# Joining the last two stages of an 8-core transformer block: no barrier between them, final-stage buffers cut from four to two, down-projection buffers cut by one

## What is computed

```python
x = x + _layernorm(_L0_attn_ref(_layernorm(x), ...))      # 16 heads of 128, rope, softmax, output projection
x = x + _layernorm(_L0_ffn_ref(_layernorm(x), ...))

def _L0_ffn_ref(x1, ...):
    w_up = dequant4bit(w_up_q, w_up_scale).T               # 2048 -> 8192
    y1 = x1 @ w_up + b_up + x1 @ w_up_lora_a @ w_up_lora_b
    x2 = jax.nn.relu(y1)
    w_down = dequant4bit(w_down_q, w_down_scale).T         # 8192 -> 2048
    y2 = x2 @ w_down + b_down + x2 @ w_down_lora_a @ w_down_lora_b
    return y2
```

## Time and profile before

| | us |
|---|---|
| timed runs (3) | 6494.24, 6898.83, 6917.61; median 6898.83 |
| profiled execution | 6499.66 |
| its span (core 5, the slowest) | 6497.6 |
| spans of the eight cores | 6372.7 to 6497.6 |
| PE busy in the span | 4829.7 (74%) |
| DVE busy | 1799.8 (28%) |
| ACT busy | 1460.6 (22%) |
| stage 7, first L963 matmul to last bias add | about 5232 to 6315 |
| stage 8, first load issued to end | about 6319 to 6497.6 |

### The profile page before, as it was taken

How to read it: one execution, slowest core, us unless ns; L and a number is a source line. 1 busy time by engine, 2 the same in 40 slices (tenths; PEclk the granted TensorE clock), 3 DMA queues, 4 the chain that set the end, 5 groups by cost and what they waited for, 6 DMA issues and landing times.

```text
span 6497.6 us, 61217 instructions; the slowest of 8 cores (6372.7 to 6497.6 us)
## 1 busy us (share of the span) xinstructions
PE 4829.7 (74%) x21121; PEld 1803.6 (28%) x21121; DVE 1799.8 (28%) x2547; ACT 1460.6 (22%) x1556; POOL 841.2 (13%) x1501
## 2 busy tenths in 40 slices
PE   0399599594999996666665365699999599969970
PEld 0144244241222221111111122244444234424430
DVE  4677321173444442222322256000000000000006
ACT  0011000011777774444444000011111100000000
POOL 1011111111122111111111000011111300020000
PEclk9999799797999998878877687899999899989985
DMA  9533533532465567777767533622223422242237
GB/s 246 184 76 77 105 77 77 95 74 47 144 181 163 170 177 160 156 165 165 160 154 156 131 113 114 115 61 73 67 67 73 136 66 82 82 147 83 82 111 277
DMA packets 672701, 794.60 MB, mean 122 GB/s; under 512 B 495824, under 2 KB 562384, under 8 KB 632832
## 3 DMA queue, kind: packets, MB, share of 16 engines
q0 software_dynamic: 117904, 463.41, 27.5%
q1 hardware_dynamic: 549888, 310.51, 18.3%
q10 hardware_dynamic: 4608, 16.78, 0.7%
HBM read 497.39 MB, written 218.24 MB: 110 GB/s over the span
## 4 chain that ended last, share of the span: by engine, by line
PE 61%; DMA 19%; DVE 9%; SPq 3%; POOL 3%; issue 3%; ACT 1%; DVEq 1%; POOLq 0%; ACTq 0%
PE pqk L377 17%; PE pu L873 14%; PE pd L963 14%; DMA sbc<-wdnsc_t 11%; SPq L98 3%; PE ps_s L600 3%; PE po L718 2%; DMA xb<-x_full 2%; PE ps_l L626 2%; PE ps_c L622 2%; PE ps_s L602 2%; DVE linv_sb L641 2%; PE ps_c L624 2%; PE pu L877 1%; ACT pbuf L618 1%
## 5 line engine op out<-in xcount | busy, mean ns | idle before, releaser
L377 PE MATMUL pqk<-wfull,ltb 128*128 128x512 bf16 x5120 | 1111.5, 380 | 407.7 <-DMA ltb<-ln1x_d 407.7
L618 ACT ACTIVATE pbuf<-ps_s,bexp_all 128x1024 bf16<-128x1024 f32 x1024 | 1135.0, 1116 | 809.7 <-PE ps_s L602 809.6
L963 PE MATMUL pd<-wd_sl,h2h 128*128 128x512 bf16 x4096 | 897.8, 383 | 65.9 <-DVE y2b L981 63.9
L873 PE MATMUL pu<-lt,wu_sl 128*128 128x512 bf16 x4096 | 928.4, 380 | 1.0 <-DVE xa_sb L846 1.0
L377 PEld LDWEIGHTS pqk<-wfull,ltb 128*128 128x128 bf16 x5120 | 502.2, 98 | 1016.5 <-issue 416.5
L600 PE MATMUL ps_s<-qtb,ktb 128*128 128x512 bf16 x1024 | 420.4, 411 | 418.9 <-DVE ctxT L650 339.5
L963 PEld LDWEIGHTS pd<-wd_sl,h2h 128*128 128x128 bf16 x4096 | 403.1, 99 | 560.6 <-issue 86.5
L873 PEld LDWEIGHTS pu<-lt,wu_sl 128*128 128x128 bf16 x4096 | 379.6, 98 | 482.3 <-issue 59.3
L622 PE MATMUL ps_c<-pbuf,vtb 128*128 128x512 bf16 x1024 | 401.4, 392 | 132.3 <-ACT pbuf L618 80.5
L718 PE MATMUL po<-wo_sb,ctxT 128*128 128x512 bf16 x1024 | 258.8, 420 | 223.6 <-DMA ob_bc<-ob_r 121.2
L602 PE MATMUL ps_s<-qtb,ktb 128*128 128x512 bf16 x1024 | 413.1, 403 | 0.0
(11 more groups left out here) (118 smaller groups left out, 3193.6 us busy)
## 6 DMA issues: line engine op xcount, KB each, us to landing
iqb<-wupq POOLq DMA_DIRECT2D x64, 1024.0 KB, 7.2
iqb<-wdnq_t POOLq DMA_DIRECT2D x64, 1024.0 KB, 13.4
sbc<-wdnsc_t POOLq DMA_DIRECT2D x128, 512.0 KB, 17.8
wd_sl<-wdn_deq_d SPq DMA_DIRECT2D x512, 128.0 KB, 2.2
xb<-x_full SPq DMA_DIRECT2D x32, 1024.0 KB, 8.7
wup_deq_d<-dqb SPq DMA_DIRECT2D x64, 512.0 KB, 3.0
wdn_deq_d<-dqb SPq DMA_DIRECT2D x64, 512.0 KB, 5.6
h_d<-h2b POOLq DMA_DIRECT2D x256, 128.0 KB, 2.0
```

The costliest lines, as they stand in the source:

```text
L377: last = e.matmul(pp[:], ltb[lp][:, dc * 512 + t1 * 128: dc * 512 + (t1 + 1) * 128], wfull[:, dc * C.D + og * 512: dc * C.D + (og + 1) * 512],
L618: P.ein("s", lambda e, sp=sp, h=h: e.activation(pbuf[sp][:], ps_s[sp][:], AF.Exp, bias=bexp_all[:, h:h + 1], scale=1.0), "sE")
L873: e.matmul(pp[:], wu_sl[wp][:, dc * 512 + hi * 128: dc * 512 + (hi + 1) * 128], lt2[:, dc * C.T_OWN + t5 * 512: dc * C.T_OWN + (t5 + 1) * ...
L963: last = e.matmul(pd[ti][:], h2h[:, hc * TH + ti * 128: hc * TH + (ti + 1) * 128], wd_sl[wp][:], start=first, stop=False)
```

## The change

- The barrier between stages 7 and 8 is taken out. In its place SP waits, ahead of the loads of tile tc, for the store of the last column group of that token tile (`p7_y2_done[tc]`).
- The buffers of stage 8 are allocated ahead of those of stage 7, so that both exist at the same time. To make room, NP8 goes from 4 to 2, the four `lnf` become one, `wd_sl` goes from 4 slots to 3, and `y2b` from 3 buffers to 2.
- The interleave of stage 8 goes from a lag of two to a lag of one.
- The identity matrix is allocated and loaded at the end of stage 2 rather than at the start, and the PE waits for it.

The core of the diff:

```diff
-    ident_sb = st.enter_context(nc.sbuf_tensor("ident_sb", [128, 128], F32))
-    P.dma("g", ident_sb[:], ident[:])
...
     fin = ExitStack()
+    ident_sb = fin.enter_context(nc.sbuf_tensor("ident_sb", [128, 128], F32))
+    dide = P.dma("g", ident_sb[:], ident[:])
...
     P.wait("t", "vE", P.val("vE"))
+    P.wait("t", "dg", dide)
     P.ein("t", lambda e: e.transpose(ntp[:], nmax[:], ident_sb[:]), "tM")
...
+    NP8 = 2
+    p8 = ExitStack()
+    y2t = [p8.enter_context(nc.sbuf_tensor(f"y2t{i}", [128, C.D], F32)) for i in range(NP8)]
+    xnt = [p8.enter_context(nc.sbuf_tensor(f"xnt{i}", [128, C.D], F32)) for i in range(NP8)]
+    lnf1 = p8.enter_context(nc.sbuf_tensor("lnf1", [128, C.D], F32))
+    lnf = [lnf1] * NP8
+    otb = [p8.enter_context(nc.sbuf_tensor(f"otb{i}", [128, C.D], F32)) for i in range(NP8)]
...
-    wd_sl = [p7.enter_context(nc.sbuf_tensor(f"wd_sl{i}", [128, 512], BF16)) for i in range(4)]
-    y2b = [p7.enter_context(nc.sbuf_tensor(f"y2b{i}", [128, 512], F32)) for i in range(3)]
+    wd_sl = [p7.enter_context(nc.sbuf_tensor(f"wd_sl{i}", [128, 512], BF16)) for i in range(3)]
+    y2b = [p7.enter_context(nc.sbuf_tensor(f"y2b{i}", [128, 512], F32)) for i in range(2)]
...
-                wp = w % 4
-                if w - 4 in wd_mm_end:
-                    P.wait("y", "tM", wd_mm_end[w - 4])
+                wp = w % 3
+                if w - 3 in wd_mm_end:
+                    P.wait("y", "tM", wd_mm_end[w - 3])
...
-                if uy - 3 in y2_st:
-                    P.wait("v", fy2[(uy - 3) % 3], y2_st[uy - 3])
-                yb = y2b[uy % 3]
+                if uy - 2 in y2_st:
+                    P.wait("v", fy2[(uy - 2) % 2], y2_st[uy - 2])
+                yb = y2b[uy % 2]
...
+        for ti in range(NTI):
+            uy = (C.OG - 1) * NTI + ti
+            p7_y2_done[th * NTI + ti] = (fy2[uy % 2], y2_st[uy])
         pds.close()
     p7.close()
-    P.barrier()
...
-    NP8 = 4
...
+        sname, sval = p7_y2_done[tc]
+        P.wait("y", sname, sval)
         dy2 = P.dma("y", y2t[p][:], y2_d[tc * 128:(tc + 1) * 128, :], sem=f8l[p])
...
     for tc in range(C.TCO):
         p8_stage1(tc)
-        if tc >= 2:
-            p8_stage2(tc - 2)
-    p8_stage2(C.TCO - 2)
+        if tc >= 1:
+            p8_stage2(tc - 1)
     p8_stage2(C.TCO - 1)
```

More of the change, by code:

```diff
@@ L893, in build_nc @@
         return nc, P, st
+    NP8 = 2
[5 more added lines that the diff above has]
+    otb = [p8.enter_context(nc.sbuf_tensor(f"otb{i}", [128, C.D], F32)) for i in range(NP8)]
+    s24c = [p8.enter_context(nc.sbuf_tensor(f"s24c{i}", [128, 6 * C.OG], F32)) for i in range(NP8)]
+    mv2c = [p8.enter_context(nc.sbuf_tensor(f"mv2c{i}", [128, 2], F32)) for i in range(NP8)]
+    sd1c = [p8.enter_context(nc.sbuf_tensor(f"sd1c{i}", [128, 1], F32)) for i in range(NP8)]
+    rs1c = [p8.enter_context(nc.sbuf_tensor(f"rs1c{i}", [128, 1], F32)) for i in range(NP8)]
+    nb1c = [p8.enter_context(nc.sbuf_tensor(f"nb1c{i}", [128, 1], F32)) for i in range(NP8)]
+    f8l = P.fam("f8l", NP8)
+    f8o = P.fam("f8o", NP8)
     p7 = ExitStack()
@@ L901, in build_nc @@
     xb_sb = p7.enter_context(nc.sbuf_tensor("xb_sb", [C.R, TH], BF16))
-    wd_sl = [p7.enter_context(nc.sbuf_tensor(f"wd_sl{i}", [128, 512], BF16)) for i in range(4)]
-    y2b = [p7.enter_context(nc.sbuf_tensor(f"y2b{i}", [128, 512], F32)) for i in range(3)]
+    wd_sl = [p7.enter_context(nc.sbuf_tensor(f"wd_sl{i}", [128, 512], BF16)) for i in range(3)]
+    y2b = [p7.enter_context(nc.sbuf_tensor(f"y2b{i}", [128, 512], F32)) for i in range(2)]
     f7i = P.fam("f7i", 1)
     f7h = P.fam("f7h", 1)
-    fwd = P.fam("fwd", 4)
-    fy2 = P.fam("fy2", 3)
+    fwd = P.fam("fwd", 3)
+    fy2 = P.fam("fy2", 2)
     P.dma_chunked("g", ad_sb, a_dn, f7i[0], 128, C.R, C.HC, max_desc=512)
@@ L915, in build_nc @@
     NTI = TH // 128
+    p7_y2_done = {}
     for th in range(2):
@@ L984, in build_nc @@
                 y2_st[uy] = P.dma("g", y2_d[th * TH + ti * 128: th * TH + (ti + 1) * 128,
-                                            dg5 * 512:(dg5 + 1) * 512], yb[:], sem=fy2[uy % 3])
+                                            dg5 * 512:(dg5 + 1) * 512], yb[:], sem=fy2[uy % 2])
             P.wait("t", "vQ", P.val("vQ"))
+        for ti in range(NTI):
+            uy = (C.OG - 1) * NTI + ti
+            p7_y2_done[th * NTI + ti] = (fy2[uy % 2], y2_st[uy])
         pds.close()
     p7.close()
-    P.barrier()
     if stop_after < 8:
+        P.barrier()
         return nc, P, st
-    NP8 = 4
[L994 to L1006, removed]
     p8_done = {}
```

## The result

The changed kernel is slower: the ratio of its time to that of the kernel before is 1.03, with a 95% interval of 1.0272 to 1.0329. About half of the executions of either kernel ran with a lower TensorE clock on one or both halves of the chip (down to a mean of 0.77 with the changed kernel, which otherwise has 0.87 to 0.89, and to 0.81 with the kernel before beside the experiments, otherwise 0.88 to 0.90) and took up to 10% longer, so the medians over all ten of each (6759.76 after, 6851.92 before) say more of those than of the kernels, and every other time, ratio and mean in this text leaves those executions out, or, where it is a mean over cores, those halves. The timed executions that are left took 6684 to 6721 us with the changed kernel beside 6494 to 6505 before, and its profiled one 6671.23 beside 6499.66.

The account below looks back on a forecast made before the run. Waits in series, not a busy engine or bandwidth, were taken to bound stage 8, and bias-add pauses to interrupt stage 7's matmuls. 135.9 + 6 - 13.8 + 3.6 + 32 + 3 + 0.6 = +167.3 on 6499.66 gave 6667 us, range 6615 to 6715.

Parts of the forecast that it names:

- the main term: Stage 8: load, statistics, normalisation and store in one circle of 19.98 us, one tile a turn, not two; +135.9 us.
- My floor for a turn of transfers that meet nothing: Stage 8: lone loads and stores shorten a turn by 0.4 us at most, -5 us in all.
- The rival with two sets that suffice: Stage 8 keeps 9.99 us a tile, next load under the current tile's work; +37, 6537 us; chance 0.06.
- The rival with much quicker lone transfers: Stage 8: load falls to 5.4 us, store to 2.7, turn 16.2; +118, 6618 us; chance 0.08.
- Neither a busy engine nor bandwidth sets its pace: Stage 8 before: DVE works 97 of 153 us, DMA share 0.70; a circle of waits in series sets the pace.
- The neighbour, +6: Stage 8: the neighbour core shares about 180 us of the stage and slows its transfers; +6 us.
- The edge: Between stages 7 and 8: early loads of tiles 0 and 1 gain 13.8 us; delayed last bias-add stores cost 3.6.
- Two y2b buffers: Stage 7: a third round of add and store in each of eight pauses, 4.0 us each; +32 us (20 to 37).
- Three weight slots: Stage 7: most weight landings stay hidden; +3 us, with waits for wd_sl only in the last column group.
- the line of 3.1: Stage 7: with three weight slots, a weight landing up to about 3.1 us costs the PE nothing.
- The identity: End of stage 2: the transpose waits for the late identity load, landing in 3.3 us; +0.6 us.
- The end: End of stage 8: one of three normalisations (4.4 us) behind the last statistics falls away, 22.5 of 26.9 us remain.

Follow-up runs that it names:

- two_sets: Kernel before with only stage 8's NP8 = 2 and a lag of one; 6614.4 and 6631.7 us against a mean of 6498.5.
- store_off_sp_four: Kernel before (four sets, lag two, barrier) with stage 8's store wait moved from SP's loads to DVE; 6482.7 and 6486.6 us beside 6506.1.
- joined: Kernel before with six y2b buffers, store wait on DVE, two of four load-buffer sets allocated ahead of stage 7, no barrier; 6460.9 and 6472.0 us beside 6506.1.
- joined_sp_wait: The kernel of joined with the store wait back on SP; ratio to the kernel before 0.9949 (0.9925 to 0.9973).
- y2b_two: Kernel before with two y2b buffers in place of three as its only edit; ratio 1.0061 (1.0032 to 1.009).
- slots_three: Kernel before with three weight slots in place of four as its only edit; 6511.5 us in one execution.
- barrier_back: Changed kernel with the barrier between stages 7 and 8 put back as its only edit; 6665.2 us in one execution.
- store_off_sp_again: Changed kernel with the store wait moved from SP's loads to the DVE instruction that reuses otb; ratio to the kernel before 1.0264 (1.0224 to 1.0304).
- store_cut: The kernel of store_off_sp_again with each store to out cut to 256 of its 2048 columns; ratio 1.0195 (1.0159 to 1.0232).
- store_on_act: Changed kernel with the stores to out issued from ACT's list in place of POOL's; 6666.4 and 6677.9 us beside 6684 to 6721.

## Why the prediction was right and where it was wrong

**The direction and the main term held.** I wrote that taking two of four sets leaves one circle of 19.98 us, which gives one tile a turn, and +135.9 for it. On three of the four odd cores of the changed kernel's trace stage 8 lasts 303.7 to 304.0 us (305.0 in the sum; with its +6, 311); core 3's 13 turns take 255.0 (259.7 in the sum), 19.62 each. My floor for a turn of transfers that meet nothing, 0.4 under that of before, is what they give: loads of 6.9 to 7.0 and stores of 4.15. two_sets makes it by this edit alone. The rival with two sets that suffice falls with the same trace: a turn with two sets takes 19.5 us, with next to no overlap, because a set is freed only by its own store. The rival with much quicker lone transfers, 5.4 us for the load and 2.7 for the store, falls too.

**"Neither a busy engine nor bandwidth sets its pace" was right, but with little behind it.** With the wait out of the way a tile takes 9.7 us in place of 10.7 (store_off_sp_four) and 9.5 in place of 10.7 (joined beside joined_sp_wait), at a DMA share of 0.85 to 0.94 on the odd cores (6330 to 6420 us of store_off_sp_four, 6320 to 6400 of joined). So the wait did set the pace, and the transfers come next, one microsecond a tile later. The sum does not hang on it, but any gain promised for a looser circle does.

**The base of stage 8.** The 9.99 us a tile and the 169.1 us were read from core 5, the quickest of the odd cores in this stage: its own mean over 13 steps is 10.11, the others have 10.6 to 10.9, and the four take 175.2 us on average. Against the mean core stage 8 grew by 131.9 us, not by 135.9 + 6. That the total of the profiled execution came out within 4 us of the sum is therefore in part luck, as the table below shows.

**The neighbour, +6.** Core 1, the slowest, has turns of 20.50 (6377.07 to 6643.60 for 13), +11 over core 3. The loads that ran at about 6370 us on cores 0, 1, 2 and 3, in this order (chains of the changed kernel, start us, us):

```profile
6367.55 7.04 DMA xnt<-xnew_d
```

```profile
6368.23 8.75 DMA xnt<-xnew_d
```

```profile
6370.38 6.91 DMA xnt<-xnew_d
```

```profile
6376.40 6.94 DMA xnt<-xnew_d
```

Cores 0 and 1 start theirs 0.7 us apart, and core 1's is 1.8 us longer; the later ones of both take 7.1 to 8.7; cores 2 and 3 start 6 us apart in the same stage and lose nothing. (Each core's times count from its own first instruction; that the cores begin together is assumed here.) So sharing the stage is not by itself what costs, as I had it. The moment at which equal turns meet fits: cores 0 and 1 load 0.7 to 5.2 us apart as long as both load, and core 1's turns are 20.2 to 21.9 us; cores 2 and 3 are 6 apart, the other pairs 9 to 10, and nearly all of their turns are 19.4 to 20.0. No run sets that distance on purpose, so this is a reading. Its size for the slowest core was of the right order. That it is this which differs from execution to execution is my reading, not shown.

**The edge.** The gap went from 13.9 to 0, as in the sum (-13.8). The price of it was under-sized: I took +3.6 for the last stores that meet the 4 MB of early loads, from the slowest landing in the earlier trace rows (4.5); the first landed after 7.8 us. The rounds behind it took up part of that: the pause is 20.9 on core 1, where 14.6 + 3.6 = 18.2 was expected, and 19.0 on the mean odd core, so the term is short by 0.8 to 2.7. A bound from a row without that company was no bound for the landing.

**Two y2b buffers.** 14.8 us a pause against 14.6 in the sum; held. Their +3.6 at the end of the kernel is in no term.

**Three weight slots.** 7.3 us in 13 waits against +3, and eight of the 13 lie outside the last column group, where I wrote there would be none. I had read the median of that time (2.2) and put the tail all into the last group. The slowest landings of those groups in the new trace, 3.5 to 3.8 on core 1, cross the line of 3.1, which was my estimate.

**The identity.** +0.1 against +0.6: it lands in 2.3 us.

**The end.** I took one normalisation (4.4) off the end of the stage. In two_sets that is what goes: from the last statistics to the end of the span it is 22.4 us against 26.9 before. In the changed kernel it is 26.1, so 3.6 of the 4.4 are not gained, and y2b_two, which keeps the four sets and the barrier, has 3.7 more than before too (30.6). So it comes with the two y2b buffers and their two semaphores, though the instructions there are those of before. The last store lands about 4 us after its issue, and what fills the rest of the 13.8 us no trace shows; why fewer buffers in stage 7 lengthen it stays open.

**The whole, and the step that failed.** The sum was +167 (6667), the profiled execution has +171.6 (6671.23). But over the executions the ratio makes it +195, and the lower end of the ratio, 1.0272, is above my 1.0257. And the median of all ten, 6759.76, lies outside 6615 to 6715. The step that failed is the base: I made the sum and the range for an execution like the profiled one, although two of the three times shown lay 6% above it, and I took one execution's spread for none. The range holds four of the five timed executions that the ratio uses, and none of the other five.

Inside the sum, the step that failed is that everything ahead of stage 7 would stay as it was, but for the identity. The two profiled executions, split by stage, mean of the odd cores (us):

| | in the sum | measured |
|---|---|---|
| ahead of stage 7 | +0.6 | +17.3 |
| stage 7 to the start of its last bias add | +38.6 | +45.7 |
| from there to the first statistics | -13.8 | -13.1 |
| stage 8 to the end | +141.9 | +131.9 |
| together | +167.3 | +181.8 |

A term of 17 us was missing, and stage 8 was put 10 too high. Stage 7 is 7 too low, of which the weights are some 5 (7.8 us of waits on the mean odd core, against +3).

The single edits say where the missing term comes in. On the mean odd core two_sets gives +126.5, y2b_two +40.0 and slots_three +5.3, together 171.8, and barrier_back, which holds all three, gives +171.8. That the two agree so closely is chance, since single cores scatter by 10 to 17 us, but the edits do add up. Taking the barrier out as well should take 5 to 8 off. It adds 21 (6654.7 to 6675.4 us), so some 27 us appear elsewhere. Between the profiled executions of before and after, 17 us appear ahead of stage 7 (its first matmul comes at 5232.3 in place of 5215.0), and more than half of that in the attention stage (from the first `ps_s` matmul to the last `ctxT` tile), whose instructions are the same: 1986 us before and 1997 after. What is left of the 27 has no trace, as the profiled execution of the changed kernel is the shortest of its six. In the traces of the six kernels without the barrier the odd cores average 1997 to 2009 us there, and in those with it 1981 to 1990; on one and the same chip it is 1981 for store_off_sp_four and 1997 for joined. The chip does not seem to make this difference: the kernel before takes 6498.5 and 6500.3 us on average on two of them. I have no mechanism by which a barrier that comes 2,700 us after that stage could matter in it. In every kernel traced the loss goes with the missing barrier; the cause stays open.

## What to carry to other kernels

Count how many buffers a stage has by what frees one: where a set is freed by its own store, follow load, compute, store and the next load around, divide by the sets that can be under way at once, and compare it with the time per tile in the trace before taking a set away. The early start of stage 8 under stage 7 paid once (5 to 8 us, and 10 with enough store buffers); half of that stage's buffers, which paid for it, were missing in every turn (19.6 to 20.5 us a tile in place of 10.1 to 10.9 on the odd cores). Before promising what a removed wait will give, ask which transfers will then run side by side (here the load went from 7.0 to 10.4 us). And compare stages over all their steps and on all cores: one step of one core would have hidden a gain of 12 us here.

## What the runs showed of the hardware that I had not expected

- A 2 MB load and a 1 MB store of one core that started within 0.1 us of each other both landed after 10.5 to 10.7 us (store_off_sp_again, medians of the odd cores); with no other transfer of their core under way they took 7.0 and 4.15 (changed kernel, core 3). A store of only 131 KB beside such a load took 6.0 us (in the same trace 2.0 to 2.2 is the median of the other stores of that size) and left the load at 7.5 to 7.6 (store_cut).
- A mix of loads and stores moved 316 GB/s at a DMA share of 0.90 (store_off_sp_four, core 5, 6350 to 6440 us). At the start of stage 8, with loads alone under way, the second tile's 2 MB were complete 5.4 us after the first's, 388 GB/s.
- The 1 MB store issued by ACT left 0.1 us after the add that it waits for and landed after 3.9 us (store_on_act); from POOL it was 0.6 and 4.15 (changed kernel, core 3).
- From the last add to the end of the span it is 10.7 us in the kernel before and 14.3 with two y2b buffers in place of three, though no instruction there differs, on all eight cores alike within 0.1 us. With six it is 9.0 to 9.6 us.
